# Last stage of a decoder layer: ScalarE rounds the q and o weights to their high part, GpSimd only subtracts

## The reference

```python
x = x + mamba(layernorm(x))                 # in_proj, conv, selective scan, out_proj
x = x + attention(layernorm(x), ctx)        # 32 query heads, 8 kv heads of 128
x = x + mixture(layernorm(x))               # 64 low-rank experts, top 16
# attention:
q = (query @ Wq).reshape(B, S, 32, 128)     # Wq 512 x 4096
k, v = key @ Wk, value @ Wv                 # 8 heads, each serves 4 query heads
q, k = rope(q), rope(k)
attn = softmax(where(mask == 0, -1e9, q @ k.T / sqrt(128)))
return (attn @ v).reshape(B, S, 4096) @ Wo  # Wo 4096 x 512
```

## Time and profile before

| what | value |
|---|---|
| median of three runs (lowest, highest) | 2364.16 us (2362.36, 2365.87) |
| the profiled execution: its time, its span | 2367.41 us, 2365.6 us |
| busy in the span: PE, DVE, ACT, POOL | 89%, 76%, 45%, 25% |
| last stage (2028 us to the end) | 338 us of the span |

### The profile page before, as it was taken

How to read it: one execution, slowest core, us unless ns; L and a number is a source line. 1 busy time by engine, 2 the same in 40 slices (tenths; PEclk the granted TensorE clock), 3 DMA queues, 4 the chain that set the end, 5 groups by cost and what they waited for, 6 DMA issues and landing times.

```text
span 2365.6 us, 27225 instructions
## 1 busy us (share of the span) xinstructions
PE 2095.8 (89%) x8272; PEld 1188.3 (50%) x8272; DVE 1802.3 (76%) x1816; ACT 1058.3 (45%) x2615; POOL 588.8 (25%) x408
## 2 busy tenths in 40 slices
PE   6877888989999979998999988998999979799988
PEld 2332453445555534445555543445555544477774
DVE  3499994389999985259999996359999995355653
ACT  2544441465555522266555542255655550243331
POOL 0089991001111111001111111001111111556650
PEclk9788999889999999989999999989999999899999
DMA  1468984238888881237888873236888874322310
GB/s 63 157 159 195 213 211 132 63 125 178 172 192 177 177 193 45 84 114 154 176 176 193 178 151 105 80 111 135 176 184 167 186 148 132 112 89 85 98 58 18
DMA packets 110121, 328.98 MB, mean 139 GB/s; under 512 B 12992, under 2 KB 13120, under 8 KB 107616
## 3 DMA queue, kind: packets, MB, share of 16 engines
q0 software_dynamic: 35328, 127.94, 29.1%
q1 hardware_dynamic: 68960, 189.58, 26.7%
q10 hardware_dynamic: 5760, 10.49, 1.2%
HBM read 183.00 MB, written 14.94 MB: 84 GB/s over the span
## 4 chain that ended last, share of the span: by engine, by line
DVE 41%; PE 31%; issue 16%; DMA 6%; ACT 4%; DVEq 1%; SPq 1%; POOL 1%; POOLq 0%; ACTq 0%; PEldq 0%
DVE hs L1170 13%; PE acc L1553 5%; DVE hs L1177 5%; DMA xc<-hs 4%; DVE hs L1342 4%; PE acc L1675 4%; DVE hs L1161 3%; PE pq L1606 2%; DVE qr L1207 2%; PE acc L1688 2%; PE acc L1767 2%; PE pq L1844 2%; PE pq L1636 2%; DVE sc L1227 2%; PE pk L1844 2%
## 5 line engine op out<-in xcount | busy, mean ns | idle before, releaser
L713 POOL DMA_DIRECT2D xc<-hs x192 | 165.8, 866 | 1305.9 <-DVE hs L1177 1269.0
L1170 DVE TENSOR_TENSOR_SCAN hs<-dA,hs 128x1024 f32<-128x1024 f32 x192 | 429.0, 2277 | 0.0
L900 ACT ACTIVATE dA<-dt,aneg 128x504 f32<-128x504 f32 x384 | 253.5, 707 | 253.6 <-DVE hs L1170 253.4
L1606 PE MATMUL pq<-qT,wa 128*128 128x512 f32 x768 | 353.8, 615 | 9.4 <-DVE sc L1227 9.4
L1688 PE MATMUL acc<-wb,oT 128*128 128x512 f32 x768 | 354.9, 607 | 3.6 <-ACT oT L888 3.6
L1177 DVE TENSOR_TENSOR hs<-hs,bc 128x1024 f32<-128x1024 f32 x256 | 308.2, 1206 | 2.2
L865 ACT ACTIVATE pr<-sc,mx 128x64 f32<-128x64 f32 x512 | 170.8, 335 | 243.1 <-DVE mx L1233 243.1
L1553 PE MATMUL acc<-xnT,wa 128*128 128x512 f32 x512 | 232.3, 607 | 12.4 <-PE acc L1553 4.7
L1606 PEld LDWEIGHTS pq<-qT,wa 128*128 128x128 f32 x768 | 146.6, 196 | 183.3 <-issue 173.1
L1161 DVE TENSOR_TENSOR hs<-u,bc 128x1024 f32<-128x1024 f32 x192 | 226.5, 1220 | 11.2 <-ACT xc L983 5.9
L1688 PEld LDWEIGHTS acc<-wb,oT 128*128 128x128 f32 x768 | 142.4, 195 | 149.7 <-issue 145.6
(11 more groups left out here) (234 smaller groups left out, 3363.5 us busy)
## 6 DMA issues: line engine op xcount, KB each, us to landing
xc<-hs POOLq DMA_DIRECT2D x240, 512.0 KB, 7.0
bc<-bc_rows SPq DMA_DIRECT2D x64, 512.0 KB, 7.5
wa<-in_wq SPq DMA_DIRECT2D x64, 512.0 KB, 9.8
wb<-in_wo SPq DMA_DIRECT2D x64, 512.0 KB, 5.2
wa<-in_wx SPq DMA_DIRECT2D x16, 512.0 KB, 4.6
wa<-in_wz SPq DMA_DIRECT2D x16, 512.0 KB, 6.1
wb<-in_ow SPq DMA_DIRECT2D x16, 512.0 KB, 6.3
k<-k_rows SPq DMA_DIRECT2D x32, 256.0 KB, 11.1
```

Source lines behind the costliest of these rows:

```text
L713: G.dma_start(xc[:, 2 * c:2 * c + 2, :], hs[:, c, :].rearrange("p (d t) -> p d t", t=T), accum_op=ALU.add).then_inc(s_y[c], 16)
L900: ins = S.activation(to[:, :, 1:SEQ], dt[:, s, :].rearrange("p (b t) -> p b t", t=SEQ)[:, :, 1:SEQ], ACT.Exp, scale=aneg[:, s, bass.ds(jj ...
L1170: V.tensor_tensor_scan(out=hs[:, c, :], data0=dA[:, c % 2, :], data1=hs[:, c, :], initial=0.0, op0=ALU.mult, op1=ALU.add).then_inc(scd.sem, 1)
L1606: ins = M.matmul(pq[:, h, :], wa4(p)[:, k, h * P:(h + 1) * P], qT[:, k, :], start=(k == 0), stop=(k == KE - 1))
```

## The change

In the last stage ScalarE makes the high parts, by an activation Copy with an fp32r output, and GpSimd waits for it and subtracts. The rounding of the q weights of n+2 stands first in ACT's step n, ahead of `evac_pt`; that of the o weights of n+1 stands between `exps` and `evac_o`. The first two tiles of q and the first of o are still made by GpSimd alone, as before. `hold` is one semaphore increment of the engine's own. The semaphores `wqh` and `woh` now count ScalarE's tiles, and `fwh` the three of GpSimd. In `split_wq` and `split_wo` the waits for the loaded tile and for the free buffer now stand only in the case that is not rounded; ScalarE has them. A raw tile is still freed after the subtraction.

```diff
-            lead(eng, ln1r, ln2r, ln3r, wqh, wqs, woh, wos)
+            lead(eng, ln1r, ln2r, ln3r, wqs, wos, fwh)
...
-                def split(raw, two, hi, both, value):
-
-                    G.tensor_scalar(two[0], raw, 1.0, None, ALU.mult).then_inc(hi.sem, 1)
-                    eng.wait_ge(hi.sem, value(hi))
+                def split(raw, two, hi, both, value, rounded):
+
+                    if not rounded:
+                        G.tensor_scalar(two[0], raw, 1.0, None, ALU.mult).then_inc(fwh.sem, 1)
+                        eng.wait_ge(fwh.sem, value(fwh))
+                    else:
+                        eng.wait_ge(hi.sem, value(hi))
+                        hold(eng)
                     G.tensor_tensor(two[1], raw, two[0].bitcast(F32), ALU.subtract).then_inc(both.sem, 1)
...
-                    split_wq(0, 0)
+                    split_wq(0, 0, False)
                     eng.wait_ge(ln2t.sem, ln2t.upto(i - 1, KE - 1))
-                    split_wq(0, 1)
-                    split_wo(0, 0)
+                    split_wq(0, 1, False)
+                    split_wo(0, 0, False)
                     steps(eng, split_step)
...
+                def round_wq(jj, o):
+                    p = o % 2
+                    eng.wait_ge(s_wa[p], (wa_half(i) + (o // 2 + 1) + jj) * 16)
+
+                    eng.wait_ge(qd.sem, qd.upto(blk, o - 2) + jj * 2)
+                    S.activation(wq2[p][0][:, :], wa[:, p, :], ACT.Copy).then_inc(wqh.sem, 1)
+
+                def round_wo(jj, o):
+                    p = o % 2
+                    eng.wait_ge(s_wb[p], (wb_half(i) + (o // 2 + 1) + jj) * 16)
+
+                    eng.wait_ge(wod.sem, wod.upto(blk, o - 2) + jj * 2)
+                    S.activation(wo2[p][0][:, :], wb[:, p, :], ACT.Copy).then_inc(woh.sem, 1)
+
                 def step(jj, p, tail):
 
                     last = tail and p == 1
+                    if not mamba and not tail:
+                        round_wq(jj, p + 2)
                     if attn:
                         evac_pt(jj, p)
...
                     if attn and not last:
                         exps(jj, p + 1)
+                    if not mamba and not last:
+                        round_wo(jj, p + 1)
                     if mamba and not last:
                         decay(jj, p + 1, 0)
```

More of the change, by code:

```diff
@@ L338, in build @@
         woh = stage("wo_hi", PAIRS)
+        fwh = stage("first_weights_hi", 3)
         wos = stage("wo_split", PAIRS)
@@ L675, in split, with split_wq @@
                     G.tensor_tensor(two[1], raw, two[0].bitcast(F32), ALU.subtract).then_inc(both.sem, 1)
-                def split_wq(jj, o):
+                def split_wq(jj, o, rounded=True):
                     p = o % 2
[L679 to L683, removed]
+                    if not rounded:
+                        eng.wait_ge(s_wa[p], (wa_half(i) + (o // 2 + 1) + jj) * 16)
+                        eng.wait_ge(qd.sem, qd.upto(i - 1, o - 2) + jj * 2)
+                        hold(eng)
+                    split(wa[:, p, :], [x[:, :] for x in wq2[p]], wqh, wqs,
+                          (lambda s: s.upto(0, o - 2) + jj * 2) if rounded else (lambda s: s.upto(0, o)), rounded)
@@ L684, in split_wq, with split_wo @@
                     eng.wait_ge(wqs.sem, wqs.upto(0, o) + jj * 2)
                     eng.sem_inc(wad, 1)
-                def split_wo(jj, o):
+                def split_wo(jj, o, rounded=True):
                     p = o % 2
[L689 to L693, removed]
+                    if not rounded:
+                        eng.wait_ge(s_wb[p], (wb_half(i) + (o // 2 + 1) + jj) * 16)
+                        eng.wait_ge(wod.sem, wod.upto(i - 1, o - 2) + jj * 2)
+                        hold(eng)
+                    split(wb[:, p, :], [x[:, :] for x in wo2[p]], woh, wos,
+                          (lambda s: s.upto(0, o - 1) + jj * 2) if rounded else (lambda s: s.upto(0, 2)), rounded)
@@ L806, in _ @@
             lead(eng, xnr, cv0, xcr, ssqd, ssr, dtv, spe, spl, dar, rop, qrd, k2r, vrdy, y0r, scf, exd, ptr, ordy,
-                 x3r, rqr, rex, zgr, szr, qTr)
+                 x3r, rqr, rex, zgr, szr, qTr, wqh, woh)
             S = nc.scalar
```

## The result

| | before | after |
|---|---|---|
| median of the runs on the same chip | 2363.26 us (4 runs) | 2407.84 us (2407.15 to 2408.18, 4 runs) |
| ratio, 95% interval | | 1.0193, 1.0177 to 1.0210 |
| span of the profiled execution | 2365.6 us | 2405.8 us |
| granted clock, mean over the span | 0.949 | 0.937 |

The kernel is 44.6 us slower. I had forecast slower, by 9.5 us, and a range that ended at 2382: the sign is right, the size is far outside. Lines have moved by 25: L1208 is now sin times the swapped q, L1211 the last subtraction of the rotation, L1661 the scores, L1623 project_q, L1700 project_o, L1687 values, L1672 the turn.

What follows compares the result with a forecast made beforehand. TensorE was taken as near its limit, with the q loop at 16.7 us a step setting the pace after the change. Terms of +8.5 us plus 1 for the clock gave 2364.2 + 9.5 = 2373.7 us, range 2361 to 2382.

Steps and rivals of the forecast that it cites:

- The o loop: Last stage: scores, exponentials, o rounding, evac_o, o_low, turn of the probabilities, next scores; put at 15.75 us a step.
- the q loop: Last stage: scores, project_q, swap_q, q rotation on VectorE, next scores; with the collision 16.84 or 16.61 us, taken as 16.7.
- The copies on ScalarE: 29 copies of 128 x 1024 in the last stage at 1.04 us each, 30 us; their place decides, not their sum.
- The collision: GpSimd's q subtraction meets VectorE's q rotation in every step, in 14 of 16 rotations; if VectorE is first, L1186 stands 2.11 us.
- I add 1: Allowance of 1 us for TensorE's clock, whose drops may come more or less often with two waits of about 1 us.
- the sum: First rotations +0.9, twelve steps +5.5, last full step +1.05, o loop ahead of the last turn +1.04: together +8.5 us.
- a rival with 0.10: TensorE's clock falls oftener: 0.65 to 1.6 us more in 12 steps, 2381 to 2392 us; chance 0.10.
- The sign that I had named: The prediction is wrong if, among other signs, TensorE's 24 matmuls often take 7 us.
- two waits of 1 us: Each step was to have two TensorE waits of about 1 us, shorter than the single waits before.
- would show with 0.65: A clock drop of 1.6 us in project_o would show with 0.65, as scores come 0.95 behind it; in project_q with 1.6.
- That the collision doesn't hold VectorE: Rival: GpSimd waits or comes too late, the o loop sets the pace; -6.4 or -1.6 us, about 2360; chance 0.15.
- Half of the steps colliding: Rival: half of the steps collide or the hold is shorter, about 16.2 us a step, +2 to +4, 2367; chance 0.12.

Runs made afterwards that it cites:

- q_sub_waits: The changed kernel with one wait more: GpSimd's subtraction of q starts only when the q rotation of the same step is done; 2361.06 us, 0.9979.
- fill: The changed kernel with 4 matmuls of zeros ahead of each turn of the probabilities and 4 ahead of each scores; 2374.03 us, 1.0040.
- both_moved: The changed kernel with GpSimd's q subtraction behind the q rotation and ScalarE's rounding of o behind evac_o; 2341.09 us, 0.9898.
- before_fill: The kernel before the change with two matmuls of zeros ahead of each turn of the probabilities; 2363.46 us, 0.9981.
- o_only: The changed kernel with only the o weights rounded by ScalarE, the q weights split on GpSimd as before; 2369.78 us, 1.0032.
- fill_one: The changed kernel with one matmul of zeros (0.2 us) ahead of each scores; 2371.27 us in three runs, once 2411.00.
- fill_first: The changed kernel with the zeros of fill in steps 1 to 3 only; 2378.83 us (2373.11 to 2396.49), 1.0075.
- fill_turn: The changed kernel with 4 matmuls of zeros ahead of each turn of the probabilities only; 2374.32 us, 1.0034.

## Why the prediction was wrong

- **The bound and the two loops.** Right at the full clock. The o loop with the rounding in it was put at 15.75 us and runs at 15.68 in q_sub_waits; the q loop with the collision was put at 16.6 to 16.8 and runs at 16.7 in fill.
- **The copies on ScalarE.** Right: 1.04 and 1.06 for 1.04, and hidden but for the place of the o rounding: q_sub_waits has 15.68 us a step, both_moved, where that rounding stands behind evac_o, 14.73.
- **The collision.** Right, in its place, its number (14 rotations) and its size (2.09 for 2.11). Its outcome is always VectorE first. The Trainium skill, page "SBUF — State Buffer", section "Who interferes with whom", says that issue order decides who blocks. The trace agrees: L1208 is issued 0.1 us ahead and keeps its 1.21, GpSimd's subtraction stands until it has ended (3.35 for 2.34), and the next VectorE instruction stands behind that.
- **The clock.** This is the step that failed, the term "I add 1". It cost 2.5 us in each of twelve steps, 30 us, and 2 in the step behind them. Without it the sum is +8.5, 2372.7 us, and fill, which takes it away, gives 2374.0. What this confirms is the twelve steps: 200.42 us in fill, 200.4 forecast. That the total agrees as well is partly luck: in fill's trace they begin 2.6 us earlier than before, where 0.9 later was forecast, and what follows them costs 5.3 more for a forecast 2.1. I had the case as a rival with 0.10, and its price (0.65 to 1.6 a step) was too low as well. The sign that I had named, 24 matmuls that often take 7, came: project_q takes 6.2 to 7.7 in every step of the chain. Two arguments were wrong. First, that the waits get shorter than the 1.9 of before: I worked with two waits of 1 us, right at the full clock only. I did not ask where they lie once a project_q has been slow, and then they are one of 2.0. Second, that a slow stretch would show with 0.65 because it falls on project_o: the wait ahead of the scores puts it on scores, values and project_q, all of the q loop, and that shows in full. The swap of q starts 10.43 us after the scores at 2142.64, where it was 8.77 at the full clock, and the rest of the loop, 7.81, is as forecast (7.84).
- **The warning in the rows.** Three project_o runs of 7.07, one of them in the earlier trace rows, each behind a wait of 1.9 us. The kernel before has six such waits in its twelve steps, and three were followed by 5.48, as the second of these:

```profile
2109.95 0.63 PE L1647 MATMUL pk<-ident,pr 128*128 128x128 f32 x4 [1.89 <-DVE oT_lo L1287]
...
2143.24 0.63 PE L1647 MATMUL pk<-ident,pr 128*128 128x128 f32 x4 [1.93 <-DVE oT_lo L1287]
```

before_fill, which leaves waits of 1.49 us and has no slow project_o, speaks for the length of these waits as the cause. So a wait of nearly 2 us brought a slow run in half of the cases. With such a wait in every step that was to be priced, and the rows had the price.
- **The rivals.** That the collision doesn't hold VectorE would have given 2360; q_sub_waits, which makes it so, gives 2361.1. Half of the steps colliding was priced at 16.2 us a step and 2367; o_only, where it is so, has 16.2 and 2369.8.

The Trainium skill, page "TensorE: Matmul & The Clock Gate", section "HAM oscillation — how this bites in real kernels", describes a matmul loop whose wait in each round has the next round start throttled, so that the cost is paid each time. The changed kernel agrees in that the cost comes back in each step, with a granted clock of 0.85. The waits of the section's kernel are for a DMA and longer than the 2.0 us here, so it would have been a reason to give that rival more, but not a price for it.

What stays open: what tips a run from one pace to the other (fill_one and fill_first do both), and what decides whether the clock falls behind a given wait. The traces show it behind every wait of 1.8 to 2.0 us ahead of the scores, behind three of six of 1.9 ahead of the turn (before), behind two of twelve of 0.7 to 1.15 (fill_turn, the two of 0.79 and 0.82), and behind none of 1.49 (before_fill).

## What to carry to other kernels

When work moves to another engine, ask what its end releases: a GpSimd instruction that reads SBUF, released by the same event as a VectorE instruction with two SBUF inputs, met it here in every round, and a wait that orders the two is free if the GpSimd instruction isn't urgent (here -47 us). When a wait is opened on TensorE's path, price it twice, once for itself and once for the matmuls behind it at the lowered clock, and ask whether these lie in the loop that sets the pace. Two waits of half the length were not the same as one here: they lowered the clock now and then, the one of 2.0 us in every step.

## What was not expected of the hardware

The same program runs in two paces. With the same collision in every step, a step takes 16.6 us at a granted clock of 1.00 with waits of 1.05 and 0.79 (one such step is in the trace of fill_first; fill, with these waits filled, has 16.7 throughout), or 18.2 to 19.8 us at 0.85 with one wait of 2.0. One matmul of zeros of 0.2 us in each step was enough to bring three of four runs to the first, and fillers in three steps alone gave seven runs spread over 23 us.
